# Macaron attention block: head and tail of the program rewritten, weight pieces redistributed, side work of the second batch in later steps

## The reference, cut to what matters

```python
# x: (4, 512, 512) f32; 32 query heads, 8 key/value groups, head size 128, causal
x = x + 0.5 * ffn(layernorm(x))
x = x + attention(layernorm(x))        # q,k,v projections, rope, softmax, Wo, bo
x = x + 0.5 * ffn(layernorm(x))

def ffn(h):
    query = h @ Wq.T
    scores = (query @ Wr.T) @ (aux_keys @ Wr.T).T / sqrt(48) + log_rel
    top_idx = top_k(scores, 8)                      # of 128 slots, per token
    w = softmax(query @ aux_keys[top_idx].T / 8 + log_rel[top_idx])
    aux = (w @ aux_values[top_idx]) @ Wvd.T @ Wvu.T
    var = variance of h;  log_var = log1p(var)
    norm_var = log_var / (mean of log_var over ALL tokens + 1e-6)
    u = clip(0.5*norm_var + 2.5*sigmoid(gelu(h@Wu1.T+bu1)@Wu2.T+bu2), 0, 5)
    gate = sigmoid(gate_w1 * clip((u-0.5)/1.5, 0, 1) + gate_bias), 0 if below 0.05
    return h + gate * aux
```

## Time and profile before

| | |
|---|---|
| median of 3 runs | 1447.65 us (1447.54 to 1447.71) |
| profiled execution | 1448.45 us |
| its span, first to last instruction | 1446.6 us |
| PE busy | 1372.6 us, 95% of the span |
| DVE, ACT, POOL busy | 80%, 65%, 56% |
| chain that ended last, by engine | PE 74%, DVE 10%, POOL 6%, ACT 4%, issue 4% |

### The profile page before, as it was taken

The page is one execution under the profiler, slowest core; times in us unless marked ns, Lnnn a source line. Parts: engine busy times, 40 slices in busy tenths (PEclk is TensorE's granted clock), DMA queues, the critical chain, the costliest instruction groups (busy, mean ns, idle before and its releaser), DMA issues.

```text
span 1446.6 us, 26790 instructions
## 1 busy us (share of the span) xinstructions
PE 1372.6 (95%) x8689; PEld 779.1 (54%) x8818; DVE 1160.3 (80%) x2854; ACT 945.4 (65%) x2440; POOL 814.0 (56%) x1177
## 2 busy tenths in 40 slices
PE   6679999998999999999999999999999999999996
PEld 4445555554555655555555655555555555555543
DVE  6888968888788877888778878889777887868655
ACT  5468677676677676666666666666766667566734
POOL 3587778788875454445645554445654465454412
PEclk9799999999999999999999999999999999999997
DMA  8656867778667566546567666557566676555433
GB/s 294 205 105 135 205 167 178 180 185 207 155 155 156 125 140 139 135 117 141 140 141 153 135 142 123 137 121 150 129 135 140 134 159 154 115 139 109 93 77 117
DMA packets 440282, 212.14 MB, mean 147 GB/s; under 512 B 382128, under 2 KB 383344, under 8 KB 440144
## 3 DMA queue, kind: packets, MB, share of 16 engines
q1 hardware_dynamic: 439168, 209.31, 62.5%
q10 hardware_dynamic: 976, 1.12, 0.2%
HBM read 91.88 MB, written 25.17 MB: 81 GB/s over the span
## 4 chain that ended last, share of the span: by engine, by line
PE 74%; DVE 10%; POOL 6%; ACT 4%; issue 4%; DMA 1%; SPq 0%; DVEq 0%; ACTq 0%
PE PJ L1301 17%; PE PJ L1302 16%; PE PJ L1300 16%; PE PV L1300 4%; PE PV L1302 4%; PE PV L1301 4%; PE SC L1475 4%; PE SC L1473 4%; PE SC L1474 4%; POOL t L575 3%; DVE phl L1106 2%; ACT p L752 2%; DVE t L1061 1%; DVE p L1096 1%; DVE t L1059 1%
## 5 line engine op out<-in xcount | busy, mean ns | idle before, releaser
L590 POOL TENSOR_TENSOR oTl<-of,oTf 128x256 f16<-128x256 f32 x256 | 171.9, 692 | 384.9 <-ACT oTf L744 384.9
L752 ACT ACTIVATE p<-p,mn 128x512 f32<-128x512 f32 (+3 forms) x512 | 280.8, 549 | 89.1 <-DVE mn L1096 89.1
L1106 DVE SCALAR_TENSOR_TENSOR phl<-p,ri,phl 128x128 f16<-128x128 f32 (+3 forms) x512 | 323.5, 672 | 0.0
L575 POOL TENSOR_TENSOR t<-t 128x256 f32<-128x256 f32 x316 | 229.1, 746 | 57.2 <-DVE t L1061 57.0
L763 ACT ACTIVATE phl<-p,ri 128x128 f16<-128x128 f32 (+3 forms) x512 | 245.6, 550 | 4.1
L1300 PE MATMUL PJ<-XT,wsp 128*128 128x512 f16 x640 | 243.6, 381 | 3.8 <-DVE t L1061 3.8
L1301 PE MATMUL PJ<-XT,wsp 128*128 128x512 f16 x640 | 243.6, 381 | 0.0
L1302 PE MATMUL PJ<-XT,wsp 128*128 128x512 f16 x640 | 243.3, 380 | 0.0
L1096 DVE CUSTOM_DVE_ANT_0 p<-SC,maskw 128x512 f32<-128x512 f32 (+3 forms) x512 | 219.7, 485 | 2.1
L580 POOL TENSOR_TENSOR qTl<-t,qTh 128x256 f16<-128x256 f32 x254 | 166.8, 677 | 92.5 <-ACT qTh L728 92.5
L1301 PE MATMUL PJ<-wosp,oTf 128*128 128x512 f16 x512 | 194.0, 379 | 4.5 <-issue 0.2
(11 more groups left out here) (221 smaller groups left out, 2651.4 us busy)
## 6 DMA issues: line engine op xcount, KB each, us to landing
wsp<-kept SPq DMA_DIRECT2D x150, 256.0 KB, 3.1
wosp<-kept SPq DMA_DIRECT2D x96, 256.0 KB, 3.5
raw<-in_wqkv SPq DMA_DIRECT2D x48, 256.0 KB, 4.8
kept<-wsp SPq DMA_DIRECT2D x42, 256.0 KB, 2.5
raw<-in_wo SPq DMA_DIRECT2D x32, 256.0 KB, 4.7
kept<-wosp SPq DMA_DIRECT2D x32, 256.0 KB, 3.1
pTf<-phl SPq DMA_TRANSPOSE x256, 3.8
X<-in_x SPq DMA_DIRECT2D x3, 1024.0 KB, 8.4
```

The costliest lines, as they stand in the source:

```text
L575: ins = nc.gpsimd.tensor_tensor(t1[:, j, c], t1[:, j, c], t2[:, j, c], ALU.add)
L590: ins = nc.gpsimd.tensor_tensor(oTl[:, n % 2, h, c], of[:, s % 2, c], oTh[:, n % 2, h, c], ALU.subtract)
L752: ins = nc.scalar.activation(pt, pt, ACT.Exp, bias=mn[:, par, i:i + 1], scale=-1.0, accum_out=rs[:, par, i:i + 1])
L1106: nc.vector.scalar_tensor_tensor(out=phl[:, par, low(i, 0):low(i, i) + 1, :], in0=p[:, par, SOFF[i]:SOFF[i] + w].rearrange("p (k t) -> p k ...
```

## The change

- **Router by tile.** In the head, scores, `take_scores`, `top` and the exponentials go by single tiles (`score_bank`). `r_sc`, `r_use`, `r_mn`, `r_e`, `r_t`, `r_hi` and `r_lo` now count tiles. ACT's `sums` are of tiles 6 to 10, and DVE's statistics of tiles 11 to 15 are between and behind the selections. Gelu stands behind the exponentials on ACT. The four matmuls that made half of a router matrix each are fused into one of 256 columns.
- **Loads.** The first two `raw` loads are issued ahead of the last X load and the small constants, the other six ahead of the rope tables.
- **Folded gates.** The division by 1.5 and the -0.5 are folded into `lmean` and `nv`, one clip goes, and the 0.05 test and its product are one operation. Two instructions fewer in `gate_2`, one in `gate_3`. `1/sm` is a step of its own (`inverse_sums`).
- **Weight pieces.** POOL makes 0 to 3, waits for the head's gates (`r_gs`), makes 4 and 5. DVE makes 6 to 10 behind `turned_lo(1, 0, 3)`. POOL waits for the first two low halves of rope and makes 11, then does its rope of Q(0,1), then 12 to 15.
- **Side work of the second batch.** `LATER` moves the `_A` rows of steps 0 to 16 one to three steps back while batch 0 is in the attention.
- **Tail.** The last adds on DVE also sum their rows, and ACT squares them. Layernorm goes by two pairs of tiles. Six matmuls whose result isn't used stand between the transposes of tiles 13 and 14. The gates of tiles 0 to 11 are computed apart and earlier, with the sigmoid done wholly on ACT (`tail_sigmoid`: Exp, Ln, Exp). Selections go as the pair 0, 1, then tile 2, then tile 3. Three of the 16 adds go through ACT and POOL, 13 are DVE's, and ACT issues the store of tile 14.

```diff
+LATER = {0: 3, 1: 4, 2: 5, 3: 6, 4: 7, 5: 8, 6: 8, 7: 9, 8: 10, 9: 11, 10: 11, 11: 12, 12: 13, 13: 14, 14: 15, 15: 16, 16: 17}
...
-        out += [(name, k, b + 1, i) for name, k, i in table_a.get(u, [])]
+        for at in sorted(table_a):
+            if (LATER.get(at, at) if b == 0 else at) == u:
+                out += [(name, k, b + 1, i) for name, k, i in table_a[at]]
...
             load_x(8, 4)
+            raw_load(0)
+            raw_load(1)
             load_x(12, 4)
...
-            for r in range(NHEAD):
+            for r in range(NSPLIT):
                 weight_low(r)
+            pool.wait_ge(r_gs[0], 1)
+            for r in range(NSPLIT, BYDVE[0]):
+                weight_low(r)
+            pool.wait_ge(rope_lo, 2)
+            pool.wait_ge(w_lo, BYDVE[-1] + 1)
+            weight_low(BYDVE[-1] + 1)
             rope("Q", 0, 1)
+            for r in range(BYDVE[-1] + 2, NHEAD):
+                weight_low(r)
...
# ACT, head
-            for n in range(BYACT + 2, NT):
-                sums(n)
+            for n in BYACT[:3]:
+                sums(n)
+            exps_ffn(0, 0, (0, 1))
+            sums(BYACT[3])
+            exps_ffn(0, 0, (2, 3))
+            sums(BYACT[4])
             act.wait_ge(ld_fs, 96)
-            gelu(0, 0, True)
-            exps_ffn(0, 0)
+            gelu(0, 0)
+            e_hi(0, 0)
...
# DVE, head, behind the second layernorm
                 turned_lo(1, 0, i)
+            for r in BYDVE:
+                weight_low(r)
...
# DVE, tail
+            gate_1(1, 0, 12, 3)
+            inverse_sums(1, 0, 12, 3)
+            project_last(0)
+            project_last(1)
+            project_last(2)
+            variance_of_squares(0, 2)
+            project_last(3)
+            deviation(2, bb, 12, 14)
+            normal(2, bb, 0)
+            normal(2, bb, 1)
+            variance_of_squares(2, 4)
...
+            select(0, 1)
+            dve.wait_ge(g_exd, 9)
+            gate_2(1, 0, 12)
+            select(2)
+            dve.wait_ge(g_exd, 10)
+            gate_3(0, 12)
+            scales(1, 0, 12)
+            select(3)
+            add(0)
+            add(2)
+            learned(1, bb)
+            gate_1(1, 12, NT, 4)
+            inverse_sums(1, 12, NT, 4)
+            add(4)
+            add(6)
...
# PE, tail
+                if task == ("LT", 2, B - 1, 2):
+                    free(task)
+                    for _ in range(6):
+                        mm(bank(task), v2h[:, 0:P], v2h[:, :], start=True, stop=True)
                 ffn_task(task)
```

More of the change, by code:

```diff
@@ L26 @@
 NROPE = 4
-BYACT = 10
+BYACT = range(6, 11)
 NSPLIT = 4
+BYDVE = range(6, 11)
 SOFF = [896, 1024, 512, 0]
@@ L495, in _ @@
                 sp.dma_start(dst, src).then_inc(ld_t, 16)
-            for r in range(4, NRAW):
-                raw_load(r)
             for r in range(NHEAD):
@@ L819, in _ @@
             root(0, 1, 4, NT)
[L820 to L823 removed]
             weight_high(7)
[L825 to L826 removed]
+            for i in range(4):
+                turned_hi(1, 0, i)
             for r in range(8, NHEAD):
@@ L864, in _, with squares @@
             out_hi(NS - 2)
+            tail_sigmoid(8, 0, 12)
             out_hi(NS - 1)
             bb = B - 1
-            root(2, bb, 4 * bb, 4 * bb + 4)
-            logs(1)
-            for i in range(4):
-                turned_hi(2, bb, i)
-            gelu(1, bb)
-            for i in range(4):
-                base(2, bb, i)
-            gate_exp(8, 0, NT)
-            gate_exp(9, 0, NT)
-            exps_ffn(1, bb)
+            def squares(i):
+                n = 4 * bb + i
+                act.wait_ge(o_add, 4 * (NU - 1) + i + 1)
+                nc.scalar.activation(t2[:, i, :], X[:, n, :], ACT.Square, bias=X[:, n, 0:1], scale=-1.0,
+                                     accum_out=z2[:, i:i + 1]).then_inc(a_z, 1)
@@ L886, in aux_odd @@
                                      scale=gs[:, 1, n:n + 1]).then_inc(r_xa[1], 1)
-            aux_odd(odd[0])
-            e_hi(1, bb)
-            for n in odd[1:]:
-                aux_odd(n)
+            for i in range(3):
+                squares(i)
+            root(2, bb, 12, 14)
+            squares(3)
+            root(2, bb + 1, 14, 16)
+            turned_hi(2, bb, 0)
+            turned_hi(2, bb, 1)
+            logs(1)
+            turned_hi(2, bb, 2)
+            turned_hi(2, bb, 3)
@@ new lines, in _ @@
+            nc.scalar.preload_act_table(ACT.Gelu_apprx_tanh)
+            for i in range(3):
+                base(2, bb, i)
+            gelu(1, bb, True)
+            tail_sigmoid(9, 0, 12)
+            exps_ffn(1, bb, (0, 1))
+            exps_ffn(1, bb, (2,))
+            aux_odd(1)
+            aux_odd(3)
+            exps_ffn(1, bb, (3,))
+            tail_sigmoid(10, 12, NT)
+            e_hi(1, bb)
+            aux_odd(5)
+            tail_sigmoid(11, 12, NT)
+            base(2, bb, 3)
@@ L904, in variance @@
             def variance(k, c0, c1):
-                dve.wait_ge(ln_m[k], c1 - 4 if k == 1 else c1)
-                for n in range(c0, c1):
+                tiles = [n for n in range(c0, c1) if k or n not in BYACT]
+                dve.wait_ge(ln_m[k], c1 - 4 if k == 1 else (c1 - len(BYACT) if k == 0 and c1 == NT else c1))
+                for n in tiles:
                     ins = nc.vector.bn_aggr(mv[:, k, n, :], st[:, k, n, :])
@@ L1259, in _, with project_last @@
                 project_add(n, i)
-            for _, n, i, _ in LAST[2:]:
-                project_add(n, i)
             bb = B - 1
-            variance(2, 4 * bb, NT)
-            deviation(2, bb, 4 * bb, NT)
-            for i in range(4):
-                normal(2, bb, i)
-            variance_logs(1)
-            base_factors(2, 4 * bb, NT)
+            def project_last(i):
+                n, t = NU - 1, 4 * bb + i
+                dve.wait_ge(s_o, 4 * n + i + 1)
+                dve.wait_ge(o_add, 4 * (n - 1) + i + 1)
+                nc.vector.scalar_tensor_tensor(out=X[:, t, :], in0=bank(("O", n, i, 0)), scalar=1.0, in1=X[:, t, :],
+                                               op0=ALU.mult, op1=ALU.add, accum_out=z1[:, i:i + 1]).then_inc(o_add, 1)
@@ L1288, in _, with select, add @@
-            e_lo(1, bb)
-            for n in (4, 6):
-                aux_add(1, 1, n - 4, 1)
-            scales(1, 12, NT, 4)
-            for n in (8, 10, 12, 13, 14, 15):
-                aux_add(1, n // 4, n % 4, 1 if n < 12 else 2)
+            log_sum(1)
+            def select(*tiles):
+                take_scores(1, bb, tiles)
+                top(1, bb, tiles)
+            def add(n):
+                aux_add(1, n // 4, n % 4, 1 if n < 12 else 2)
+            log_mean(1)
+            select(0, 1)
@@ L1295, in _ @@
+            gate_3(12, NT)
+            scales(1, 12, NT)
+            for n in range(8, NT):
+                add(n)
         @block.tensor
@@ L1493, in _ @@
             pe.wait_ge(fs_lo, 4)
+            for task in HEAD[4:6]:
+                ffn_task(task)
+            pe.wait_ge(fs_ul, 1)
+            ffn_task(HEAD[6])
             pe.wait_ge(ld_fv, 48)
@@ L1532, in _ @@
             pe.wait_ge(o_lo, NS - 2)
-            for task in LAST[2:]:
+            for task in LAST[2:4]:
                 free(task)
```

339 lines of the change are left out of this document (191 added, 148 removed).

## The result

| | before | with the change |
|---|---|---|
| median of 20 runs | 1446.97 us (1443.37 to 1448.03) | 1449.41 us (1447.94 to 1450.92) |
| ratio | | 1.002 (95% interval 1.0014 to 1.0027) |
| profiled execution | 1448.45 us | 1448.44 us |
| its span | 1446.6 us | 1446.6 us |

The change makes the kernel slower by 0.2%, where 12.3 us less were forecast. The kernel before scatters by almost 5 us from run to run, and its profiled execution lies near the upper end. The changed kernel's lies near the lower end of its own runs. The two spans are equal by chance, which makes the traces easy to compare: whatever one place gains, another has lost.

The account below looks back on a forecast made before the run. PE bounds the middle, so only head, first steps and tail could move, the stores bounding the end: -1.3 - 3.5 - 7.5 = -12.3 from 1448.45, less 0.8 for the median, gave 1435.4 us, range 1428 to 1442.

Parts of the forecast that it names:

- First steps: Start of attention: a new wait of PE against old waits and low clock removed, -3.5 us, bounds -6 and +1.
- The new wait: Step 1, ahead of group 1's keys: PE waits 5.0 us for the kept pieces, +6.7 with half clock behind it.
- T: Start of the scores of step 0, the time from which the first steps' delays are counted.
- the old waits and the low clock: PE's waits in 60 to 130 us, 10.3, and 3.4 of half speed: 10.2 of 13.7 us were to go.
- the old wait of step 3: First steps: PE's 5.3 us wait for the transposed probabilities, to be partly replaced by the wait for kept pieces.
- steps 6 to 40: Small waits that move about: term 0, bounds -1.5 and +1.5.
- Head: Up to the scores of step 0: gates 3.0 later, rope stall 4.5 shorter, -1.3 us, ends -4.5 and +1.
- The stall: Head: DVE's first rope addition, 5.18 us beside POOL, would take 0.69, which is -4.5.
- the five subtractions: Head: DVE's weight pieces, 3.4 us, would fall into its 3.62 us wait for the first key and cost nothing.
- Tail: From the last adds and statistics to the end: earlier first store and last add, -7.5 us, ends -4.5 and -9.5.
- The third rival: Head: POOL's pieces stall DVE's five subtractions, +6.6 in all, 1454 us; chance 0.04.
- a fill worse than its bound: First steps losing more than their +1 bound; with the second rival's rest beyond 1444.8 it made up same, chance 0.04.

Follow-up runs that it names:

- e1: Changed kernel with LATER emptied, so batch 1's side work stands in its old steps: 1444.23 us, ratio 0.9981 to the kernel before.
- e2: Changed kernel, LATER kept, but POOL makes pieces 4 to 15 ahead of its first rope and DVE makes none: 1444.54 us, 0.9985 to the kernel before.
- e3: Changed kernel with LATER emptied and POOL making pieces 4 to 15 ahead of its first rope: 1442.57 us, ratio 0.9967 to the kernel before.
- e8: e2 with other steps in LATER, keeping low halves out of step 5 and the gates' work out of step 13: 1444.65 us.
- e5: e3 with gelu ahead of the exponentials of tiles 2 and 3 on ACT in the head: 1442.19 us.
- e9: e5 with the hidden layer's output product ahead on PE and DVE's u1T copy ahead of its last three statistics: 1440.22 us, 0.9959 to the kernel before.
- e6: e3 without the six unused matmuls between the transposes of tiles 13 and 14: 1443.66 us.
- e10: e9 with 23 unused matmuls in PE's tail wait ahead of the products for tiles 4 to 6: 1437.97 us, 0.9944 to the kernel before.
- e7: e3 with 23 unused matmuls in PE's tail wait ahead of the products for tiles 4 to 6: 1440.89 us.
- e12: e10 with POOL's three tail additions waiting until DVE's last selection is done: 1438.24 us.
- e4: Kernel before with LATER alone: 1446.38 us, ratio 0.9995 to the kernel before.
- e11: Kernel before, with POOL starting its last four head pieces only after DVE's first two rope additions: 1444.82 us, ratio 0.9988.

## Why the prediction was wrong

- **First steps, the step that failed.** Forecast -3.5, measured +5.3, in two parts of about equal size: +1.0 up to step 6, where -3.5 was forecast, and +4.3 behind it, where the term was 0.
- *Up to step 6.* The new wait had its cause and place right. POOL ended at 75.5, T + 10.9 where T + 11.2 was worked out, and the loads were issued 1.0 later. It lasted 7.8 instead of 5.0, since five loads follow each other and PE starts 6.2 us after the first issue, just beyond the upper bound of 6.0 and not at the median of 3.3 that I took. The 1.7 of half clock behind it, for which the prediction shows no row, came: PE's granted clock is 0.50 until about 86.1. So the new wait cost 9.5 and not 6.7. Against it some 8.5 of the old waits and the low clock went, and not the 10.2 of the sum. That the old wait of step 3 would be absorbed was right (5.3 became 0.8), but the new wait does this by itself (0.7 in e1). From step 0 to step 6 `LATER` gains 3.7 without the hold-back (e2 against e3) and 0.5 with it (the changed kernel against e1), so there was little left for it to gain.
- *Behind step 6.* What failed here is the sentence that `LATER` puts work "into steps 3 to 6, where PE waits little". I took little waiting for room. The kernel before shows no wait in steps 6 to 12, and with the moved work in these steps waits of 4.0 stand in steps 7 and 13, with a lower clock behind them. The low half of 1.35 on POOL ahead of a key's rope is one part of the first; PE's own moved work is another, and without that low half (e8) 2.1 remain and others appear. I also stopped at step 6, although `LATER` reaches step 17, and gave steps 6 to 40 a term of 0. By e1 to e3 `LATER` costs 2.0 alone and 5.2 with the hold-back, and the hold-back 1.7 and 4.9.
- **Head.** Forecast -1.3, measured -0.3. The stall went as forecast (-4.5) and the five subtractions were hidden. The gates came 4.7 later, not 3.0, just outside my bound of 4.5; in e1, with the same head, they came 3.6 later and step 0 was 1.1 ahead, so much of this miss is scatter between traces. The chain I summed (exponentials, sums, two table loads) is real, but e5 shows that it wasn't the only one: the value product, behind which the output product stands, ended at the same time. I had not followed PE's order there, nor DVE's, which took over three statistics (e9).
- **Tail.** Forecast -7.5, measured -5.0. To the first selection -4.0 (forecast -4.1, in which the clock's part was 1.3 by e6, not 2.2). From there to the first add -2.9 (forecast -3.6): two DVE instructions were held up by POOL for 1.9 together. From the first add to the last 13.9 us instead of 10.2 before; I had 11.6, or 13.6 with the low clock, and took a value nearer the better end. The low clock was there, and e10 against e9 prices it at 2.1 (e7 against e3: 1.8). From the last add to the end 4.8 (forecast 4.6).
- The Trainium skill, page "TensorE: Matmul & The Clock Gate", section "Part 4: PE-mode transpose", was weighed for the tail. In e6 the clock stands at 0.50 behind idle time and transposes; in the changed kernel, with six ordinary matmuls between the transposes, it stands at 1.00. The runs agree with the page but don't part idle time from transposes.
- The third rival, DVE's subtractions held up by POOL, did not occur. POOL was done with piece 5 at 45.5. A stall beside POOL turned up in the tail, where I had not looked for it. The Trainium skill, page "SBUF — State Buffer", section "Who interferes with whom", states it also for VectorE instructions with one input in a two-port mode. The runs agree that not only two-input ones are held up: the first of the two instructions and the one that e12 shows at 1.12 are TENSOR_SCALAR with one tile as input, and without POOL beside it the first falls from 1.15 to 0.23. The second, from 1.25 to 0.29, reads two tiles. No run here shows which mode they are in.
- No change, or slower, had 0.08 in my chances. The case that happened, the moved work costing more where it went than it freed, was none of my rivals; the nearest was "a fill worse than its bound", without a mechanism. Nor was it bad luck: all three terms were off to the same side.

## What to carry to other kernels

A step without waits isn't a step with room: before side work is moved, follow the queue of the engine that does it through the new place, past each instruction that another engine waits for, as far as the move reaches. Move the bound engine's own side work only with the waits in view that it covers. Time in which that engine waits anyway, as in a pipeline's fill, need not be cleared: here clearing it bought nothing on the kernel before (e4) and cost 2.0 on e3. When a cost has been found on one chain, look for a second that ends at the same time: e5 took 4.1 us from one and the first X update came 0.25 earlier.

## What the runs showed of the hardware

- A DVE instruction on 4 columns (0.17 us) took 1.12 us beside two POOL additions (e12), and one on 128 columns 1.15 instead of 0.23 (changed kernel). Both lost 0.9 us, so the loss didn't shrink with the instruction.
- Without the stall in the head (e11) 4.4 us at step 0 were 2.7 from step 3 on: the first steps passed on an earlier start in part, and in e9 the whole 1.2.
- Unused matmuls in PE's idle time bought 1.3 us in one gap (e6) and 2.1 in another (e10 against e9), through the granted clock of the real ones behind them, 1.00 instead of 0.50.
